# Attention 2: one stretch of value products per key tile, behind both maximum products and all four scores

## The reference

```
Q = (query @ Wq.T).reshape(B, QL, HEADS, HEAD_DIM)        # HEADS, HEAD_DIM = 16, 16
K = kv_k.reshape(KV, HEADS, HEAD_DIM)                     # KV = 4096
V = kv_v.reshape(KV, HEADS, HEAD_DIM)
scores = jnp.einsum('bqhd,khd->bhqk', Q, K) * SCALE
attn = jax.nn.softmax(scores, axis=-1)
out = jnp.einsum('bhqk,khd->bqhd', attn, V).reshape(B, QL, HIDDEN)
return out @ Wo.T
```

## Time and profile before

| | |
|---|---|
| median of 3 runs | 2233.84 us |
| profiled execution, device time | 2250.17 us |
| its span, first to last instruction | 2248.4 us |
| TensorE, VectorE, ScalarE busy | 90%, 70%, 61% of the span |
| mean granted TensorE clock | 0.930 of full speed |

### The profile page before, as it was taken

The page is one execution under the profiler, slowest core; times in us unless marked ns, Lnnn a source line. Parts: engine busy times, 40 slices in busy tenths (PEclk is TensorE's granted clock), DMA queues, the critical chain, the costliest instruction groups (busy, mean ns, idle before and its releaser), DMA issues. The chain is left out here.

```text
span 2248.4 us, 40077 instructions
## 1 busy us (share of the span) xinstructions
PE 2017.5 (90%) x15956; PEld 1006.2 (45%) x15956; DVE 1573.8 (70%) x1951; ACT 1361.0 (61%) x2700; POOL 260.1 (12%) x274
## 2 busy tenths in 40 slices
PE   6793999992478999999999999999999999999984
PEld 3552889991222333333333333333333333446663
DVE  2337212215587999998999999999999999315344
ACT  1220444440114888887888888888888888673221
POOL 0000434431020000000000000000000000002462
PEclk9795999995665999999999999999999999999997
DMA  4201677765815000006100006000002000001124
GB/s 139 84 5 66 211 227 255 254 193 138 107 45 69 6 9 13 13 1 69 13 1 14 13 1 69 13 2 13 13 18 64 2 2 1 17 16 34 59 83 154
DMA packets 150034, 140.93 MB, mean 63 GB/s; under 512 B 75506, under 2 KB 122590, under 8 KB 149086
## 3 DMA queue, kind: packets, MB, share of 16 engines
q1 hardware_dynamic: 140446, 112.72, 21.3%
q0 software_dynamic: 9408, 25.70, 3.5%
HBM read 106.40 MB, written 31.72 MB: 61 GB/s over the span
## 5 line engine op out<-in xcount | busy, mean ns | idle before, releaser
L1003 DVE TENSOR_REDUCE maxp<-banks 128x2 f32<-128x1024 f32 x1024 | 1241.2, 1224 | 73.8 <-PE banks L997 72.8
L1435 ACT ACTIVATE pring<-banks 128x512 f32<-128x512 f32 x2048 | 1108.4, 595 | 231.1 <-PE banks L1316 117.6
L1330 PE MATMUL banks<-pring,vcur 128*17 128x256 f32 x8192 | 650.8, 390 | 7.9 <-ACT osb L1429 3.6
L1316 PE MATMUL banks<-qst,kst 50*128 50x512 f32 x2048 | 523.6, 502 | 6.9 <-PEq L1074 5.4
L997 PE MATMUL banks<-kst,qst 48*128 48x512 f32 x2048 | 438.5, 426 | 29.6 <-DVE maxp L1003 26.4
L1316 PEld LDWEIGHTS banks<-qst,kst 50*128 50x128 f32 x2048 | 199.3, 185 | 448.7 <-ACT pring L1435 416.4
L1330 PEld LDWEIGHTS banks<-pring,vcur 128*17 128x17 f32 x8192 | 137.1, 96 | 369.2 <-issue 202.6
L997 PEld LDWEIGHTS banks<-kst,qst 48*128 48x128 f32 x2048 | 202.1, 194 | 76.7 <-DVE maxp L1003 68.8
L766 ACT ACTIVATE hT<-banks,b 128x128 f32<-128x128 f32 x295 | 108.1, 367 | 187.8 <-PE banks L703 172.2
L904 DVE TENSOR_SCALAR yo<-banks,wblock 128x256 f32<-128x256 f32 x59 | 28.5, 484 | 223.8 <-PE banks L712 223.8
L1301 POOL TENSOR_TENSOR acc<-xn,orec 128x256 f32<-128x256 f32 x15 | 9.3, 620 | 1254.9 <-DVE orec L1480 1254.9
(11 more groups left out here) (304 smaller groups left out, 1306.0 us busy)
## 6 DMA issues: line engine op xcount, KB each, us to landing
w1r<-in_L_ffn_w SPq DMA_DIRECT2D x59, 640.0 KB
kst<-key_parts SPq DMA_DIRECT2D x24, 512.0 KB, 17.6
key_parts<-ksp SPq DMA_DIRECT2D x32, 256.0 KB
w2all<-in_L_ffn_w SPq DMA_DIRECT2D x12, 640.0 KB, 7.7
w2all<-expert_rows SPq DMA_DIRECT2D x12, 512.0 KB, 8.7
qst<-query_parts SPq DMA_DIRECT2D x96, 64.0 KB, 2.3
normed_rows<-xn SPq DMA_DIRECT2D x8, 512.0 KB, 2.9
kf<-in_kT SPq DMA_DIRECT2D x16, 256.0 KB
```

The source lines that it names most:

```text
L1003: return nc.vector.tensor_reduce(maxp[:, B % 2, :, hp, qt, kb], ps[:, base:base + 2, :], X, ALU.max)
L1316: nc.tensor.matmul(ps[:, n % 3, :], kst[g % 2][rows, j // 2, kt * P:(kt + 1) * P], qst[i][rows, j // 2, :], start=True, stop=True).then_in ...
L1330: mm = nc.tensor.matmul(ps[32 * j:32 * j + VC, 7, cols], vcur[g % 2][:, kt, j, :], pring[:, (G % 2) * HG + j, cols], start=(kt == 0 and ha ...
L1435: nc.scalar.activation(pring[:, n % (2 * HG), :], ps[:, n % 3, :], ACT.Exp, scale=float(DH) ** -0.5).then_inc(exp_done, 1)
```

## The change

The order of TensorE's work within a step. Before, in a step: scores 0 and 1, first list of units, values half 0, scores 2 and 3, second list, values half 1. After: scores 0 and 1, first list, second list, scores 2 and 3, values half 0, values half 1. The instructions, their operands, their waits and the other engines' queues are the same.

```diff
@@ -1390,13 +1390,12 @@
                         scores(B, kt, 1)
                         for e in one:
                             unit(*e)
+                        for e in two:
+                            unit(*e)
+                        scores(B, kt, 2)
+                        scores(B, kt, 3)
                         if G:
                             values(G - 1, 0)
-                        scores(B, kt, 2)
-                        scores(B, kt, 3)
-                        for e in two:
-                            unit(*e)
-                        if G:
                             values(G - 1, 1)
                     values(BATCHES * NKT - 1, 0)
                     values(BATCHES * NKT - 1, 1)
```

## The result

The changed kernel takes **2305.75 us** in the median of four runs (2297.94 to 2307.61); the kernel before, beside it, 2233.39 (2232.63 to 2234.01). The ratio is **1.0317**, with a 95% interval of 1.0294 to 1.0341: 72 us slower. The forecast was 2329, 2298 to 2365.

A forecast was written before the change was run, and what follows sets the result against it. TensorE and VectorE were taken to be full and at the same pace. Terms of +90 (batches 1 to 13), +6, +5, -1 and -5 gave +95 us on 2233.84: 2329 us, range 2298 to 2365.

The forecast's parts named there:

- The plain step: Ordinary step of the second attention: score 3 waits for score 0's exponential, so 2.62 us against 2.44, +0.175 us.
- The rival that the second half of the values pays a switch: Second half of the values costs 0.33 instead of 0.22 behind the first: +45 us, 2374 in all; chance 0.05.
- The gain on TensorE: Going in and out of the values once instead of twice per step: TensorE's own work 2.1 us against 2.44.
- the score wait: Score 3 may not start before 1.18 us behind score 0, whose exponential it needs; two max units cover only 0.77.
- The sum: All batches, ends and half-clock steps of the second attention together: +95 us, 2329 us in all.
- the special steps: Steps 1, 2, 3, 29 and 30 of a batch, with transposes or copies: together +2.17 us a batch.
- Step 2: Transposes of the sums wait for the bank of the step's first unit: 4.08 us against 3.39, +0.69.
- Step 29: Transpose of the maxima comes no sooner than 2.29 us, scores and all values behind it: 3.93 against 3.05, +0.88.
- Steps 3 and 30: ScalarE's copies come behind or beside exponentials and delay the next one: +0.42 and +0.18 us.
- Batch 0 and the last batch: Ends of the second attention: batch 0 +5 us, with -2.5 from some six half-clock steps; last batch -1.
- The half-clock term: Some eight more steps at 1.2 GHz fall from 4.28 to 3.8 us: -5 us.
- The clock rival: TensorE's short idles make its clock swing; one step in ten at 3.8 us gives +57, about 2386; chance 0.06.

The follow-up runs named there:

- experiment 2: Changed kernel with the second list of units moved behind scores 2 and 3, all values still last: 1.0729 times the kernel before.
- experiment 3: Changed kernel with each reduction over 256 instead of 512 columns of a bank: 1.0189 times the kernel before.
- experiment 4: Changed kernel with each exponential over 256 of the 512 queries: 0.9986 times the kernel before.
- experiment 5: Four kernels with one-product max units, against the kernel before: new order with three score banks 1.0224, four 0.9251; old order with three 1.0040, four 1.0021.
- experiment 1: Changed kernel with values half 0 put back between the units and scores 2 and 3: 1.0641 times the kernel before.
- experiment 9: Changed kernel with values half 0 back ahead of scores 2 and 3, and exponentials over 256 of 512 queries: 1.039 times the kernel before.
- experiment 7: Kernel before with only the transposes of the sums put ahead of the units in step 2: 1.0016 times the kernel before.

## Why the prediction was right

**The plain step.** Forecast 2.62, measured 2.60. Each term is in the trace: score 3 at 1.18, 0.43 to the values, 0.23 and twice 0.22 between their fours, and 0.33 back. The forecast had 1.01 for the values where they take 0.99. The rival that the second half of the values pays a switch is out with that. Experiments 2 to 5 leave no other cause: less cover makes it longer by what was taken (2.83), less VectorE doesn't change it (2.60), a shorter exponential or a fourth bank ends it (2.42 in the mean, 2.12).

**The gain on TensorE.** 2.1 us without the wait, measured 2.12. That it could not be had was the core of the forecast. The Trainium skill, TensorEngine Tiling (Array Packing), section Key Properties, states that a change of the tiling mode drains TensorE. Experiment 5 agrees: 0.32 us a step for two changes saved and the weight loads that they made late; how the 0.32 divides between these two no run shows.

**VectorE.** I had its wait under the score wait with 0.2 us to spare. Experiment 3 bears it out. The trace shows a little more room than that: the second unit started 0.58 us into the step (1703.38) where I had 0.65, and score 2 after 0.92 (1703.72) where I had 0.98, since two reductions behind an idle stretch took 2.36 us instead of 2.45. VectorE idles 0.25 us a step for that reason, not 0.17.

**The sum was too large: +95 against +72, or +79 in the stage.** Profile against profile, by first exponentials of each batch:

| | forecast | measured |
|---|---|---|
| batches 1 to 13, full clock | +90 | +73 (80.26 to 85.88, each) |
| batch 14 | +6 | +5 |
| batch 0 | +5 | -1 |
| last batch | -1 | +8 |
| half-clock and other single long steps in batches 1 to 13 | -5 | -7 |

Of the 1.3 us a batch in the first row, 0.5 is the 0.02 of the plain step and the rest the special steps, forecast at +2.2 us together and measured at +1.4. Step 2 was right (4.08, measured 4.06). Step 29, in TensorE's timeline at the place of the earlier trace rows:

```profile
856.56 0.50 PE L1316 MATMUL banks<-qst,kst 50*128 50x512 f32 x2
...
858.62 0.28 PE L1376 MATMUL banks<-ident,mneg 128*16 128x128 f32 x1 [0.97 <-DVE maxp L1003]
...
860.24 0.50 PE L1316 MATMUL banks<-qst,kst 50*128 50x512 f32 x2
```

It was put at 3.93 on the ground that its transpose comes no sooner than 2.29 us into the step; it came after 2.06 (856.56 to 858.62), released by the reduction of the step's first unit, because VectorE, idle now, had the total of the maxima done earlier: 3.68. That step of my working failed: I carried over a time from a kernel in which VectorE was full. Steps 3 and 30 were put at 2.86 and 2.76 and took 2.65 and 2.60. There I laid ScalarE's exponentials and copies end to end by their lengths, 0.60 and 0.59. They overlap: here the first of two exponentials and the copy behind them start 0.97 apart, and the next exponential 0.46 behind the copy.

```profile
873.92 1.08 ACT L1434 ACTIVATE pring<-banks 128x512 f32<-128x512 f32 x2 [1.56 <-PE banks L1316]
874.89 0.59 ACT L1421 COPY xn<-banks 128x512 f32<-128x512 f32 x1
875.35 1.61 ACT L1434 ACTIVATE pring<-banks 128x512 f32<-128x512 f32 x3
```

Batch 0 and the last batch are the clock: it rose after two steps of batch 0 instead of seven, and stood at half in the last batch's end, where five steps took some 7 us more than in the kernel of experiment 5 that ran them at full clock. One is 6 us below the forecast, the other 9 above; that they nearly cancel is luck.

The half-clock term came out near its size by luck as well. I had eight steps of 3.8 us each. In batches 1 to 13 the clock stood at half for 17 us in the kernel before, but only for 7 in the changed one, and the one plain step wholly inside that took 4.00 us, with score 3 1.48 behind score 0: I had assumed that the wait grows little at half clock. That makes about -4.6; the rest of the -7 lies in single long steps at full clock, three before and two after. One in each kernel waited for the load of the maxima into the query tile (1.45 us before, 0.98 after); in the others TensorE stood idle, for 2.3 us in the longest, and the trace names no wait.

The clock rival did not come: both stages have a mean of 0.98, and batch 2 stood at 1.00 with its two waits per step. Experiments 1 and 9 did show a swing of the kind that it describes, in a neighbouring order and in batch 0 above all (last section).

**A hole that did not show.** I checked one way round the ring of score banks (score 0 to score 3) and not the other (score 2 to the next score 1). In the changed order all the values lie on the second, so nothing depended on it; experiment 1 did, and its forecast failed by 0.1 us a step in the plain ones. Steps 2, 3, 29 and 30, which I had not worked out, came 0.3 to 0.5 us longer than in the changed kernel.

## What to carry to other kernels

Before moving work in a hand-written order, list every wait on the engine, and for each the work that lies between it and what releases it, round the loop and in both directions; the work taken out of one gap must leave it longer than the release takes (here 1.18 us from a product through an exponential to the third product on). Fewer switches of the array's layout are worth something only while the engine has nothing to wait for. An engine that becomes idle changes the timing of its waits elsewhere too, so durations and release times measured while it was full may not carry over (here a transpose came 0.23 us sooner than I had carried over, and pairs of reductions took 2.36 us instead of 2.45).

## What the runs showed that I had not expected

**The start of the attention at half clock.** The granted clock was 0.5, 1.2 GHz, when this stage's steps began, in every profile. It rose after two or three steps in the changed kernel, with half reductions and with the new order and four banks; after seven in the kernel before and in experiment 7, which has its order. With max units of one product it stayed at 0.5 through nearly all of batch 0 or longer in three of the four kernels: 131 us for batch 0 with the new order and three banks, 137 us with the old order and either number of banks, against 79 us with the new order and four, whose steps were the shortest. Before it rose, a plain step took 4.04 us in the first of these kernels, 4.27 in the two with the old order, and the one that the fourth did wholly at half clock took 3.79. That is why those three ratios say less than the steps do. What decides it I have not tested.

**A clock that swings.** In experiment 1 the clock rose after four steps, and then fell and rose four more times within batch 0; 73 of its 121 us stood at 0.5. In experiment 9, with the same order, it fell five times in batch 0, and 50 of 110 us stood at 0.5. None of the other kernels fell back in batch 0 once its clock had risen. Both have half of the values on either side of the second pair. Why that order swings and the changed one does not, with two waits a step as well, is open.

**A wait can cost less than it is long.** In experiment 3 the second unit no longer waited (0.02 us, and 0.1 for its late weights), score 2 came 0.12 us earlier in the step, and nothing was gained: of two waits in a row, only the one that ends last counts, though both stand in the list of waits.
